# A two-layer vision block: the first mixer as straight code, with norms on ScalarE and the routing of one group inside the turn of the next

## The chip, the cores and the metric

The kernel runs on one core of a Trainium2 chip. The metric is the device time in microseconds of one execution. Five engines work at once: TensorE (PE; its weight loads are listed as PEld), VectorE (DVE), ScalarE (ACT), GpSimd (POOL) and SyncE (SP), which only issues DMAs. They meet through semaphores: one engine adds to a semaphore when an instruction is done, another waits until it has reached a number. Each engine works through its own list in order, so that whatever stands behind a waiting instruction waits too.

## The reference

The input is x, 16 images of 32 x 32 pixels with 96 channels. Two layers follow each other. Each has a token mixer and a feed-forward part with four experts, and both are added to their input.

```python
# layer 0, mixer (what this change is about)
xn = layernorm(x, eps 1e-6)
# along the rows of the image, and again along its columns:
y    = xn @ W1.T + b1                     # 96 -> 2 numbers per pixel
z    = grouped_mix(y, W2, b2, 8)          # 1024 logits for each column (row)
attn = softmax(z.reshape(..., 32, 32))    # a 32x32 matrix for each column (row)
h, w = attn @ v                           # v: values
x = x + projection of (pixel's own product + h + w)
# layer 0, feed-forward: 4 experts, the best 2 per pixel
g = softmax(layernorm(x, eps 1e-5) @ gate_w + gate_b);  keep 2, renormalise
x = x + sum over the two of  g_e * (gelu(xn @ w1[e] + b1[e]) @ w2[e] + b2[e])
# layer 1: a state-space mixer with a 3x3 convolution, then such a feed-forward
```

## The kernel before, in words

A *group* is four images. The 128 partitions hold 4 images x 32 image columns; the free dimension holds the 32 image rows, each with 96 channels and 8 more columns (the gate scores, the two gates, mean, reciprocal deviation, pixel number). All four groups stay in SBUF as `held_rows` (called `residual` in the profile); `xr` is its first 96 columns, `xsc` its first 100. Work on 4 image rows is a *quad*; a group has NQ = 8 quads.

**First mixer.** For each group VectorE computes 32 row sums (L408), GpSimd raises the variance to the power -1/2 (L424), VectorE normalises 32 rows (L376), TensorE transposes them (L981) and multiplies them by `rhs0`, 208 columns wide: 100 value columns, 100 columns of the pixel's own product, 4 columns for the logits and 4 scores (L996). ScalarE evacuates both (L782, L790). VectorE prepares the 2 + 2 mixing columns (L1605 to L1607), transposes the values in blocks of 32 (L1609) and adds the own product to the rows (L1612). TensorE makes the logits of the two directions, m = 0 and m = 1 (L1006). For each m VectorE takes the largest (L1616) and subtracts it (L1617), ScalarE takes the exponential (L795), VectorE sums, inverts, multiplies and transposes (L1619 to L1622). TensorE then applies the matrices with 32x32 products on quarters of its array, 8 quads for m = 0, whose results ScalarE evacuates, and 8 quads for m = 1, which VectorE adds to the rows (L1021, L1629). Last, VectorE transposes the column result (L1634) and adds it (L1635). On TensorE, ScalarE and VectorE the groups are a hardware loop (`Fori`). VectorE computes the row sums of group g+1 ahead of the adds of group g and normalises its rows between them. TensorE's transposes of group g+1 come after all mixing of group g. GpSimd splits the expert weights into two parts after each power (`expert_parts`), two of eight at a time, and SyncE writes them to memory.

**Routing.** When the mixer has ended, `stage_end` is raised. SyncE loads tables (L524, L525). For each group VectorE computes 32 row sums (L1668 to L1676), GpSimd the power (L627), VectorE the scores, the choice of two of four experts and the gates (`gated`, L1687 to L1728, with one exponential on ScalarE, L802), TensorE the ranks of the tokens (L1034, L1035), and VectorE the slots (`placed`, L1735 to L1743). Then GpSimd starts 32 scatters, one per image row (L632), that write the rows into the region of their expert pair in memory. The last row sums give the plan, by which SyncE writes fill rows (L532) and ScalarE loads the weights of the first tiles (L825). The order on VectorE is: row sums 0 and 1, then for each g gating, placing, row sums g+2. GpSimd's is: powers 0 and 1, then for each g the scatters, and the power of g+2 behind them.

**Expert tiles, second mixer, expert tiles.** SyncE waits for all scatters (L539) and loads the first tile of 512 tokens (L548). 74 tiles follow, then the second mixer, whose norms are on ScalarE already (L916) and which routes as it goes (scatters L738), then 74 tiles again.

Of the kernel before, what the change touches and what calls it, by code (L numbers as in the profile page):

```python
# [5 lines left out]
ALU = mybir.AluOpType  # L6
ACT = mybir.ActivationFunctionType
AX = mybir.AxisListType
# [5 lines left out]
P = 128  # L14
# [11 lines left out]
NV = 2 * DS + 2 * E0 + NEXP  # L26
# [46 lines left out]
CHAIN_MIX0 = 54  # L73


# [6 lines left out]
class Chain:  # L82
# [16 lines left out]

    def enter(self, i, per):  # L100
        self.start = self.base + self.n
        self.base, self.n = i * per + self.start, 0

    def leave(self, rounds, per):
        assert self.n == per, (self.n, per)
        self.base, self.n = self.start + rounds * per, 0


def metaformer(nc, inp, out):
    with ExitStack() as ctx:  # L110
# [44 lines left out]
        ids = xn_flat[:, 0:P].bitcast(I32)  # L155
        pad_rows = xn_flat[:, P:P + Q * ROW].rearrange("p (q n) -> p q n", q=Q)
# [28 lines left out]
        top[0] = 0  # L185
        wc = part(D + 1)
# [4 lines left out]
        xt0 = part(2 * BANK)  # L191
        vc = part(SIDE, NV)
        vh = part(SIDE, DS)
        oh = early[:, 2 * (WROW - 2):2 * (WROW - 2) + SIDE * DS].rearrange("p (a b) -> p a b", b=DS)
        gate_end = 2 * (WROW - 2) + SIDE * DS
        gwt0, gtmp0 = (early[:, gate_end + n * NEXP * D:gate_end + (n + 1) * NEXP * D].rearrange("p (e d) -> p e d", d=D) for n in range(2))
# [3 lines left out]
        row_max = part(SIDE)  # L200
# [7 lines left out]


        top[0] = 0  # L210
        plan = part(3, TILES).bitcast(I32)
        counts = part(NPAIR).bitcast(I32)
        plan_end = top[0]
# [16 lines left out]
        slot = part(G, SIDE).bitcast(U32)  # L230
# [8 lines left out]
        table_end = top[0]  # L239
# [7 lines left out]
        top[0] = max(top[0], table_end)  # L247
# [70 lines left out]
        m_ln, m_b01_pe, m_b01_ev = sem("m_ln"), sem("m_b01_pe"), sem("m_b01_ev")  # L318
        m_v_pe, m_v_ev, m_yb, m_yt_pe, m_yt_ev = (sem(n) for n in ("m_v_pe", "m_v_ev", "m_yb", "m_yt_pe", "m_yt_ev"))
        m_z_pe, m_sub, m_exp, m_at, m_w_pe, m_w_add = (sem(n) for n in ("m_z_pe", "m_sub", "m_exp", "m_at", "m_w_pe", "m_w_add"))  # L320

# [45 lines left out]
        def layer_norm(dve, ch, src, dst, n, width, which_eps, count, ready, part=None, own=None, rows=None):  # L367
            if part != 1:
                row_stats(dve, ch, src, n, width, which_eps, own or token_norm)
            if part == 0:  # L370
                return
            _, mom, _, has_rstd = own or token_norm
            dve.wait_ge(has_rstd, count)
            mo = mom[:, :, 0:n]
            for r in rows or range(n):
                i = dve.tensor_scalar(dst(r), src(r), mo[:, 0, r:r + 1], mo[:, 5, r:r + 1], ALU.subtract, ALU.mult)  # L376
                if ready is not None and (r + 1) % Q == 0:
                    i.then_inc(ready, 1)

# [24 lines left out]

        def row_stats(dve, ch, src, n, width, which_eps, own):
            sums, mom, has_var, _ = own
            for r in range(n):
                i = dve.bn_stats(sums[:, r, :], src(r))  # L408
                ch.done(i)
            ch.wait()  # L410
            sv = sums[:, 0:n, :]
            mo = mom[:, :, 0:n]
            ch.done(dve.tensor_tensor(mo[:, 0, :], sv[:, :, 1], sv[:, :, 4], ALU.add))
            ch.done(dve.tensor_tensor(mo[:, 1, :], sv[:, :, 1], sv[:, :, 4], ALU.subtract))
            ch.link(dve.tensor_tensor(mo[:, 2, :], sv[:, :, 2], sv[:, :, 5], ALU.add))
            ch.done(dve.tensor_scalar(mo[:, 0, :], mo[:, 0, :], 0.5, None, ALU.mult))
            ch.link(dve.tensor_tensor(mo[:, 1, :], mo[:, 1, :], mo[:, 1, :], ALU.mult))
            ch.link(dve.scalar_tensor_tensor(mo[:, 3, :], mo[:, 1, :], width / 4.0, mo[:, 2, :], ALU.mult, ALU.add))
            dve.tensor_scalar(mo[:, 4, :], mo[:, 3, :], 1.0 / width, which_eps, ALU.mult, ALU.add).then_inc(has_var, 1)

        def rstd(pool, n, count, own=None):
            _, mom, has_var, has_rstd = own or token_norm
            pool.wait_ge(has_var, count)
            pool.tensor_tensor(mom[:, 5, 0:n], mom[:, 4, 0:n], half_neg[:, 0:n], ALU.pow).then_inc(has_rstd, 1)  # L424

# [49 lines left out]
        def _(sp_):  # L475
            sp_.dma_start(consts[:, :], inp["consts"]).then_inc(const_in, 16)
            for g in range(G):
# [5 lines left out]
                if g == 0:  # L483
# [5 lines left out]
                    sp_.dma_start(rhs0[0:D + 1, 2 * DS:2 * DS + 2 * E0], inp["W1T"]).then_inc(mix_in, 16)  # L489
# [4 lines left out]
                    for m in range(2):  # L494
                        for c in range(SEG):
                            sp_.dma_start(w2z[8 * c:8 * c + 8, m, c * P:(c + 1) * P], inp["W2T"][m, c]).then_inc(mix_in, 16)
                        sp_.dma_start(w2z[64:65, m, :], inp["b2z"][m]).then_inc(mix_in, 16)
# [25 lines left out]
            def route_inputs():  # L523
                sp_.dma_start(route_consts, inp["route"]).then_inc(rc_in, 16)  # L524
                sp_.dma_start(ids, inp["ids"]).then_inc(rc_in, 16)  # L525

            def pads(l):
                sp_.wait_ge(rt["plan"], l + 1)
                sp_.wait_ge(pads_set, l + 1)
# [72 lines left out]
        def _(pool):  # L602
# [21 lines left out]
            def route():  # L624
# [16 lines left out]
                for g in range(G):  # L641
                    scatter(g)
                    if g + 2 < G:
                        powers(g + 2)
# [1226 lines left out]
```

## Time and profile before

| | us |
|---|---|
| median of three timed runs | 2229.65 (2222.31 to 2231.4) |
| the profiled execution | 2230.16, its span 2228.3, mean granted TensorE clock 0.882 |
| first mixer | 0 to 295 |
| routing | 295 to 496 |
| all the rest | 496 to 2228 |

| engine | busy us | share of the span |
|---|---|---|
| PE | 1744.2 | 78% |
| DVE | 1616.2 | 73% |
| ACT | 1108.5 | 50% |
| POOL | 1278.5 | 57% |

The shares are means over stages with different limits; the change touches the first two stages alone. A granted clock of 1 is 2.4 GHz, 0.50 is 1.2 GHz.

### The profile page before, as it was taken

The numbers are of one execution on the slowest core, as the hardware profiler recorded it, in microseconds if no ns is written. First come the engines' busy times: TensorE is split into PE (matmuls) and PEld (weight loads), VectorE is DVE, ScalarE is ACT, GpSimd is POOL, SyncE is SP. The second block draws the span as 40 slices with busy tenths as digits, with TensorE's granted clock in tenths as the row PEclk, the third lists the DMA queues.
The fourth block names the chain that finished last, engine by engine and source line by source line (L and its number), as shares of the span: only waits on it lengthen the run. The fifth ranks groups of instructions, "written<-read, shape, count | busy, mean of one in ns | idle before, by whom it ended". The sixth has DMA issues, their size and how long they took to land.

```text
span 2228.3 us, 65452 instructions
## 1 busy us (share of the span) xinstructions
PE 1744.2 (78%) x25602; PEld 1397.1 (63%) x25602; DVE 1616.2 (73%) x5205; ACT 1108.5 (50%) x2124; POOL 1278.5 (57%) x1346
## 2 busy tenths in 40 slices
PE   3566610009999994899999999999999936999997
PEld 2445510007777773788878777877788724777775
DVE  3877883206777776578898989898989864777775
ACT  2223300007777774565555555545554315777775
POOL 2210147764787776344546565656666664777776
PEclk9767765559999997899999999999999857999998
DMA  9200001315555554400000000000000014555553
GB/s 146 72 23 2 25 18 37 128 54 160 181 182 187 190 191 100 60 4 3 3 3 11 11 10 11 11 11 10 10 10 12 12 39 163 189 182 192 185 184 107
DMA packets 95635, 174.31 MB, mean 78 GB/s; under 512 B 53602, under 2 KB 66939, under 8 KB 95348
## 3 DMA queue, kind: packets, MB, share of 16 engines
q10 hardware_dynamic: 21312, 102.00, 13.8%
q1 hardware_dynamic: 56372, 42.14, 8.3%
q0 software_dynamic: 17664, 26.27, 3.5%
q8 instruction: 189, 3.10, 0.6%
q14 instruction: 98, 0.80, 0.1%
HBM read 134.99 MB, written 37.31 MB: 77 GB/s over the span
## 4 chain that ended last, share of the span: by engine, by line
PE 53%; DVE 22%; issue 11%; POOL 8%; ACT 4%; DMA 1%; SPq 1%; DVEq 0%; ACTq 0%; POOLq 0%
PE ps L1026 10%; PE ps L1027 9%; PE ps L1028 9%; PE ps L1118 6%; POOL rows L632 6%; PE ps L1153 3%; PE ps L1167 2%; PE ps L1076 2%; PE ps L996 2%; PE ps L1189 1%; PE ps L1048 1%; ACT rounded L870 1%; PE ps L1164 1%; PE ps L1172 1%; PE ps L1121 1%
## 5 line engine op out<-in xcount | busy, mean ns | idle before, releaser
L1026 PE MATMUL ps<-rounded 97*128 97x512 f32 (+2 forms) x952 | 394.0, 414 | 4.5 <-DVE rounded L1770 2.8
L1027 PE MATMUL ps<-rounded 97*128 97x512 f32 (+2 forms) x952 | 377.0, 396 | 0.0
L1028 PE MATMUL ps<-rounded 97*128 97x512 f32 (+2 forms) x952 | 376.4, 395 | 0.0
L1118 PE MATMUL ps<-rounded 128*128 128x224 f32 (+1 forms) x2256 | 353.6, 299 | 4.4 <-ACT rounded L870 4.4
L848 ACT ACTIVATE rounded<-ps 128x512 fp32r<-128x512 f32 x444 | 267.2, 602 | 162.2 <-PE ps L1028 154.7
L1118 PEld LDWEIGHTS ps<-rounded 128*128 128x128 f32 x2256 | 307.9, 200 | 38.7 <-issue 8.8
L1805 DVE TENSOR_TENSOR rounded<-arena,rounded 128x512 fp32r<-128x512 f32 x296 | 222.0, 750 | 136.2 <-ACT arena L849 136.0
L664 POOL TENSOR_TENSOR rounded<-arena,rounded 128x512 fp32r<-128x512 f32 x148 | 192.7, 1302 | 160.9 <-ACT arena L849 157.9
L849 ACT ACTIVATE arena<-ps 128x512 f32<-128x512 f32 x444 | 267.1, 602 | 0.0
L710 POOL TENSOR_TENSOR w<-arena,consts 128x384 f32<-128x384 f32 x128 | 107.7, 841 | 219.8 <-DVE arena L1327 219.8
L1026 PEld LDWEIGHTS ps<-rounded 97*128 97x128 f32 (+2 forms) x952 | 166.7, 175 | 57.8 <-issue 10.4
L1028 PEld LDWEIGHTS ps<-rounded 97*128 97x128 f32 (+2 forms) x952 | 166.6, 175 | 55.6 <-issue 0.2
L1027 PEld LDWEIGHTS ps<-rounded 97*128 97x128 f32 (+2 forms) x952 | 168.8, 177 | 43.3
L1784 DVE SCALAR_TENSOR_TENSOR arena<-ps,arena 128x96 f32<-128x96 f32 x592 | 146.4, 309 | 60.4 <-PE ps L1076 60.2
L655 POOL DMA_INDIRECT after_ffn<-arena x148 | 161.9, 1094 | 35.6 <-issue 30.4
L655 POOL DMA_INDIRECT out<-arena x148 | 156.2, 1055 | 35.6 <-issue 28.7
L870 ACT CAST rounded<-rounded 96x992 fp32r<-96x992 f32 (+2 forms) x192 | 155.5, 810 | 6.6 <-DVE rounded L1331 3.9
L632 POOL DMA_INDIRECT rows<-residual,arena x128 | 123.6, 966 | 42.8 <-issue 38.4
L738 POOL DMA_INDIRECT rows<-residual,w x128 | 128.7, 1005 | 32.2 <-issue 28.8
L1765 DVE TENSOR_SCALAR arena<-arena 128x96 f32<-128x96 f32 x296 | 79.2, 333 | 86.9 <-DMA arena<-rows 68.1
L1167 PEld LDWEIGHTS ps<-arena 32*32 32x32 f32 x12288 | 133.3, 105 | 12.4 <-issue 1.4
L1048 PE MATMUL ps<-consts,arena 128*96 128x128 f32 x296 | 45.7, 278 | 113.9 <-DVE arena L1765 81.3
(309 smaller groups left out, 3816.0 us busy)
## 6 DMA issues: line engine op xcount, KB each, us to landing
rounded<-weights_by_expert ACTq DMA_DIRECT2D x148, 673.0 KB, 4.6
arena<-rows SPq DMA_DIRECT2D x74, 208.0 KB, 2.7
residual<-in_x SPq DMA_DIRECT2D x16, 384.0 KB, 7.1
weights_by_expert<-rounded SPq DMA_DIRECT2D x8, 672.0 KB, 3.2
residual<-after_ffn SPq DMA_DIRECT2D x12, 384.0 KB, 6.8
rows<-xn SPq DMA_DIRECT2D x17, 208.0 KB, 8.3
after_ffn<-arena POOLq DMA_INDIRECT x148
out<-arena POOLq DMA_INDIRECT x148
```

What stands on the lines that cost most here:

```text
L632: pool.indirect_dma_start(rows, bass.IndirectOffsetOnAxis(ap=slot[:, g, h:h + 1], axis=0), held_rows[:, g, h, :], None).then_inc(r_out[g % ...
L655: pool.indirect_dma_start(to, bass.IndirectOffsetOnAxis(ap=mine[:, COL_ID:COL_ID + 1].bitcast(U32), axis=0), mine[:, 0:D], None, bounds_ch ...
L664: pool.tensor_tensor(hidr[:, 1, c, :], hid[:, step % HIDS, :], hidr[:, 0, c, :].bitcast(F32), ALU.subtract).then_inc(f["low_pool"], 1)
L848: act.activation(hidr[:, 0, c, :], bank(UPS[step % len(UPS)]), ACT.Gelu)
L849: act.activation(hid[:, step % HIDS, :], bank(UPS[step % len(UPS)]), ACT.Gelu).then_inc(f["gelu"], 1)
L870: return act.copy(dst[:, :, :, to], src[:, :, :, frm].bitcast(F32))
L1026: pe.matmul(dst, left[0], right[0], start=start, stop=False)
L1027: pe.matmul(dst, left[1], right[0], start=False, stop=False)
L1028: return pe.matmul(dst, left[0], right[1], start=False, stop=stop)
L1118: pe.matmul(dst[:, 0:w], x3[:, x_part, n, slot, tokens], wtap[:, w_part, n, y + 1, 0:w], start=(y == 0 and n == x_part == w_part == 0), st ...
L1167: ins = pe.matmul(bank(5)[pb, n * HD:(n + 1) * HD], mm[pb, i % 2, n, :], xdt[pb, c % 2, j, n, :], start=True, stop=True)
L1805: dve.tensor_tensor(hidr[:, 1, c, :], hid[:, step % HIDS, :], hidr[:, 0, c, :].bitcast(F32), ALU.subtract).then_inc(f["low"], 1)
```

## The change

The first mixer and the routing become one piece of straight code.

- **Norms.** VectorE computes signed sums (the mean times -1); GpSimd makes the power and one product; ScalarE normalises all 32 rows of a group with a scale and a bias per row. `xt0` now holds a whole group.
- **Products.** The value product is 108 columns wide (`VC`: values, 4 logit columns, 4 scores). The other 100 columns are multiplied in the row mixing: each row of a quad is one product of full height and then four quarter products into the same PSUM columns. VectorE's separate addition (L1612) is gone. 
- **Order.** TensorE: for each group column mixing, row mixing, then columns, values and logits of the next group. ScalarE takes one exponential, evacuates two quads, takes the other, evacuates the rest, then norms, columns and values of the next group. Row sums are one group further ahead.
- **Routing of g-1 in the turn of g.** Row sums between the two softmax halves, gating before the row adds, placing after the first two; the ranks on TensorE after the second quad. GpSimd's scatters have the other powers put between them at fixed places. Its first norms and the weight splitting are reordered. The tables are loaded at the start.
- Waits at the start are split: the first products wait for 8 small loads and not for all 26.

```diff
@@ ScalarE
+            def normalise(g):
+                act.wait_ge(rstd_ready, g + 1)
+                need(act, m_t_pe, g * NQ)
+                for h in range(SIDE):
+                    ins = act.activation(xn[:, h, :], xr[:, g, h, :], ACT.Identity, bias=moments[:, 1, h:h + 1], scale=moments[:, 5, h:h + 1])
...
+            for g in range(G):
+                softmax_exp(g, 0)
+                mixed_columns(g, 0)
+                mixed_columns(g, 1)
+                softmax_exp(g, 1)
+                for q in range(2, NQ):
+                    mixed_columns(g, q)
+                if g:
+                    gate_exp(g - 1)
+                if g + 1 < G:
+                    normalise(g + 1)
+                    columns_and_values(g + 1)
+                    mixing_columns(g + 1)
+            gate_exp(G - 1)
@@ TensorE
+            def mix_rows(g, q):
+                k = g * NQ + q
+                if q == 0:
+                    pe.wait_ge(m_at, 2 * g + 2)
+                    pe.wait_ge(m_v_ev, k + NQ)
+                elif q >= 2:
+                    pe.wait_ge(m_w_add, k - 1)
+                apart()
+                for i in range(Q):
+                    h, dst = Q * q + i, bank(2 + q % 2)[:, i * DS:(i + 1) * DS]
+                    pe.matmul(dst, xt0[0:D + 1, h * P:(h + 1) * P], rhs0[0:D + 1, VC:NV], start=True, stop=False)
+                    for pb in quarter:
+                        ins = pe.matmul(dst[pb, :], at[pb, 1, :, h], vc[pb, h, 0:DS], start=False, stop=True)
+                ins.then_inc(m_w_pe, 1)
...
+            for g in range(G):
+                for q in range(NQ):
+                    mix_columns(g, q)
+                for q in range(NQ):
+                    mix_rows(g, q)
+                    if q == 1 and g:
+                        ranks_of(g - 1)
+                if g + 1 < G:
+                    columns_and_values(g + 1)
+                    mixing_weights(g + 1)
+            ranks_of(G - 1)
@@ GpSimd
+            norm_of(0)
...
+            norm_of(1)
+            parts_of(0, 1, 2, 3)
+            norm_of(2)
+            parts_of(4, 5)
+            powers(0)
+            parts_of(6, 7)
             for g in range(G):
-                rstd(pool, SIDE, g + 1)
-                for k in (2 * g, 2 * g + 1):
-                    expert_parts(k // NEXP, k % NEXP)
-            route()
+                cuts = (22, 26) if g == 0 else (26, 26) if g == 1 else (16, 16)
+                scatter_group(g, range(0, cuts[0]))
+                if g == 0:
+                    norm_of(3)
+                scatter_group(g, range(*cuts))
+                if g + 1 < G:
+                    powers(g + 1)
+                scatter_group(g, range(cuts[1], SIDE))
@@ VectorE
+            def values(g):
+                dve.wait_ge(m_v_ev, (g + 1) * NQ)
...
+            for g in range(G):
+                peaks(g, 0)
+                below_peaks(g, 0)
+                peaks(g, 1)
+                shares(g, 0)
+                below_peaks(g, 1)
+                if g:
+                    row_sums(g - 1)
+                shares(g, 1)
+                if g:
+                    gated(g - 1)
+                add_rows(g, range(2))
+                if g:
+                    placed(g - 1)
+                add_rows(g, range(2, NQ))
+                add_columns(g)
+                if g + 1 < G:
+                    values(g + 1)
+                if g + 2 < G:
+                    next_sums(g + 2)
+            dve.sem_inc(stage_end, 1)
+            row_sums(G - 1)
+            gated(G - 1)
+            placed(G - 1)
+            planned(carry, rc0)
```

`row_sums`, `gated` and `placed` have the same instructions as before. `peaks` is L1616, `below_peaks` L1617, `shares` L1619 to L1622 for one m, `add_rows` L1629, `add_columns` L1634 and L1635, `values` L1605 to L1611 without L1612, `next_sums` the 32 row sums of a later group.

## Rows read from the trace of the kernel before

**Rows 1.** Stretches of all engines: busy us (instructions) of each, clock, DMA share, GB/s.

```profile
0.00:295.00 295.00, 159.08 (x2474) 132.10 (x2474) 214.34 (x414) 79.57 (x144) 49.29 (x47) 0.79 0.24 51
295.00:496.00 201.00, 6.56 (x16) 4.56 (x16) 68.15 (x349) 1.25 (x4) 146.19 (x135) 0.50 0.18 62
```

**Rows 2.** Timeline of the scatters: start, us, engine, line, operation, idle before it.

```profile
320.84 1.19 POOL L632 DMA_INDIRECT rows<-residual,arena  x1 [4.39 <-DVEq L1744]
...
361.31 5.50 POOL L627 TENSOR_TENSOR residual<-arena,half_neg 128x32 f32<-128x32 f32 x1
...
492.98 0.95 POOL L632 DMA_INDIRECT rows<-residual,arena  x1 [0.30 <-issue]
...
496.01 42.89 SPq L548 DMA_DIRECT2D arena<-rows  x7
```

**Rows 3.** Timeline of VectorE in the routing.

```profile
310.73 0.40 DVE L1687 TENSOR_TENSOR arena<-residual 128x128 f32<-128x128 f32 x1
...
317.74 0.55 DVE L1735 TENSOR_TENSOR_SCAN arena<-xn,ps 128x192 f32<-128x192 f32 x1
...
320.63 5.21 DVE L1668 BATCH_NORM_STATS2 arena<-residual 128x6 f32<-128x96 f32 x32
...
327.05 0.40 DVE L1687 TENSOR_TENSOR arena<-residual 128x128 f32<-128x128 f32 x1
```

**Rows 4.** A stretch of all engines in the first loads (columns as Rows 1).

```profile
12.00:15.00 3.00, 0.00 (x0) 0.00 (x0) 0.00 (x0) 0.00 (x0) 0.00 (x0) 1.00 0.31 72
```

**Rows 5.** Timeline of VectorE in the first group.

```profile
19.48 0.21 DVE L1586 COPY arena<-arena 96x96 f32<-96x96 f32 x1 [17.44 <-DMA arena<-in_b2z]
...
25.11 5.21 DVE L408 BATCH_NORM_STATS2 stats<-residual 128x6 f32<-128x96 f32 x32 [0.24 <-DVE arena L365]
...
56.92 0.22 DVE L1605 COPY arena<-arena 128x64 f32<-128x64 f32 x1 [11.94 <-ACT arena L790]
```

**Rows 6.** Timeline of ScalarE in the second mixer, four norms (one alone: 450 ns).

```profile
1326.18 1.54 ACT L916 ACTIVATE xn<-residual,moments 128x96 f32<-128x96 f32 x4
```

**Rows 7.** Timeline of VectorE in a softmax of group 3.

```profile
261.36 1.22 DVE L1616 TENSOR_REDUCE arena<-ps 128x32 f32<-128x1024 f32 x1
...
269.04 1.19 DVE L1616 TENSOR_REDUCE arena<-ps 128x32 f32<-128x1024 f32 x1
```

**Rows 8.** Groups by line, 0 to 540 us: count, busy us, mean ns, idle before.

```profile
L376 DVE TENSOR_SCALAR xn<-residual,moments 128x96 f32 (+1 forms) x128 | 38.7, 368 | 19.3 <-POOL moments L424 19.3
...
L1634 DVE STREAM_TRANSPOSE arena<-early 128x3200 f32<-128x3200 f32 x4 | 23.9, 5968 | 0.0
...
L1629 DVE TENSOR_TENSOR residual<-residual,ps 128x400 f32 (+1 forms) x32 | 17.7, 562 | 3.8 <-PE ps L1021 3.4
...
L1635 DVE TENSOR_TENSOR residual<-residual,arena 128x3200 f32 (+1 forms) x4 | 14.0, 3492 | 0.1
```

**Rows 9.** Timeline of TensorE in the second mixer.

```profile
1300.29 0.64 PE L1099 MATMUL ps<-consts,xn 128*96 128x128 f32 x4
1300.87 0.26 PE L1150 MATMUL ps<-arena 16*32 16x32 f32 x8
1301.06 0.91 PE L1153 MATMUL ps<-w,consts 128*128 128x384 f32 x2
...
1305.07 2.03 PE L1189 MATMUL ps<-arena 96*128 96x100 f32 x16
1307.03 0.26 PE L1150 MATMUL ps<-arena 16*32 16x32 f32 x8
```

**Rows 10.** Timeline of TensorE in the last row mixing.

```profile
279.49 4.98 PE L1021 MATMUL ps<-arena 32*32 32x100 f32 x192 [0.16 <-DVE residual L1629]
```

**Rows 11.** A stretch of L1021 alone: PE busy, PEld busy, clock, DMA share, GB/s.

```profile
204.00:208.00 4.00, 2.59 (x64) 2.56 (x64) 0.50 0.00 0
```

**Rows 12.** The page's costliest groups: the scatters of both mixers.

```profile
L632 POOL DMA_INDIRECT rows<-residual,arena x128 | 123.6, 966 | 42.8 <-issue 38.4
L738 POOL DMA_INDIRECT rows<-residual,w x128 | 128.7, 1005 | 32.2 <-issue 28.8
```

More of the change, by code:

```diff
@@ L185, in metaformer @@
         top[0] = 0
+        plan = part(3, TILES).bitcast(I32)
+        counts = part(NPAIR).bitcast(I32)
+        plan_end = top[0]
+        slot = part(G, SIDE).bitcast(U32)
         wc = part(D + 1)
@@ new lines, in to_columns, with values @@
+            def to_columns(g, q):
+                k = g * NQ + q
+                pe.wait_ge(m_ln, k + 1)
+                if g and q == 0:
+                    pe.wait_ge(m_h_ev, k)
+                need(pe, m_t_ev, k - 1)
+                for i in range(Q):
+                    ins = pe.transpose(bank(q % 2)[0:D, i * P:(i + 1) * P], xn[:, Q * q + i, :], ident)
+                ins.then_inc(m_t_pe, 1)
+            def values(g, q):
+                k = g * NQ + q
+                pe.wait_ge(m_t_ev, k + 1)
+                need(pe, m_v_ev, k - 1)
+                if q == 0:
+                    need(pe, m_w_add, k)
+                for i in range(Q):
+                    h = Q * q + i
+                    ins = pe.matmul(bank(2 + q % 2)[:, i * VC:(i + 1) * VC], xt0[0:D + 1, h * P:(h + 1) * P], rhs0[0:D + 1, 0:VC], start=True, stop=True)
+                ins.then_inc(m_v_pe, 1)
@@ L998, in _, with columns_and_values, mixing_weights @@
+            def columns_and_values(g):
+                for q in range(NQ + 1):
+                    if q < NQ:
+                        to_columns(g, q)
+                    if q:
+                        values(g, q - 1)
+            def mixing_weights(g):
                 pe.wait_ge(m_yb, g + 1)
@@ L1594, in _ @@
+            ch.link(dve.tensor_tensor(rhs0[D:D + 1, VC:VC + D], bank(5)[D:D + 1, 0:D], bo[D:D + 1, :], ALU.add))
+            times_gates(dve, ch, rhs0[0:D + 1, VC + D:NV], rhs0[0:D + 1, VC:VC + D], gwt0, gtmp0)
             dve.sem_inc(prep_done, 1)
-            dve.sem_inc(m_w_add, NQ)
-            def normalise(g, part=None, rows=None):
-                if part != 1:
-                    dve.wait_ge(x_in, g * 64 + 64)
-                layer_norm(dve, ch, lambda r: xr[:, g, r, :], lambda r: xn[:, r, :], SIDE, D, 1e-6, g + 1, m_ln, part, rows=rows)
@@ new lines, in logits, with peaks, below_peaks @@
+            def logits(m):
+                return bank(6 - 2 * m, 2).rearrange("p (i j) -> p i j", j=SIDE)
+            def peaks(g, m):
+                dve.wait_ge(m_z_pe, g * 2 + m + 1)
+                ch.done(dve.tensor_reduce(row_max[:, m, :], logits(m), AX.X, ALU.max))
+            def below_peaks(g, m):
+                ch.wait()
+                need(dve, m_at, g * 2 + m)
+                dve.tensor_tensor(sc[:, :, :], logits(m), row_max[:, m, :].unsqueeze(2).to_broadcast([P, SIDE, SIDE]), ALU.subtract).then_inc(m_sub, 1)
@@ new lines, in shares, with add_rows @@
+            def shares(g, m):
+                dve.wait_ge(m_exp, g * 2 + m + 1)
+                ch.link(dve.tensor_reduce(row_sum, at[:, m, :, :], AX.X, ALU.add))
+                ch.link(dve.reciprocal(row_inv, row_sum))
+                ch.link(dve.tensor_tensor(sc[:, :, :], at[:, m, :, :], row_inv.unsqueeze(2).to_broadcast([P, SIDE, SIDE]), ALU.mult))
+                dve.transpose(at[:, m, :, :], sc[:, :, :]).then_inc(m_at, 1)
+            def add_rows(g, some):
+                ch.wait()
+                for q in some:
+                    dve.wait_ge(m_w_pe, g * NQ + q + 1)
```

505 lines of the change are left out of this document (214 added, 291 removed).

## The prediction

> **What bounds the kernel now.** I first cut the span into stages [rows 1]. To 295 us the first mixer runs; VectorE is busy for 214 of these 295 us, TensorE for 159 at a mean granted clock of 0.79. From 295 to 496 us the routing runs, and there only GpSimd works (146 of 201 us); TensorE does 6.6 us. Both stages are whole in the chain of waits, and the expert tiles begin only when the second has ended. I then read GpSimd's timeline in the second stage [rows 2]: the first of 128 scatters starts at 320.84, 32 of them take 40.5 us (1.265 each), a power of 5.5 us stands between two groups, and the last starts at 492.98. SyncE's load of the first tile follows at 496.01. So 320.8 to 493.9 is one engine's queue, which needs nothing but slots. VectorE has the slots of a group after 32 row sums, gating and placing: 6.4, 7.0 and 2.9 us [rows 3].
>
> **The change, part by part.** The sum is made on the profiled execution (2230.16 us; the median of the three timed runs, 2229.65, is 0.5 less). The stage after the scatters is not touched and is moved as a block; the price is therefore where the last scatter ends, against 493.9.
>
> *Start.* The waits for the mixing weights no longer stand ahead of the first row sums. DMA's share falls to 0.31 in 12 to 15 us, so the first group's rows are there at about 12.9 [rows 4]. Sums 6.4 [rows 3], power 5.5 [rows 2] and GpSimd's short product some 0.3: 25.1. The weights' preparation (5.6 us on VectorE, 19.48 to 25.11 [rows 5]) lies under the power. The longer memset of the ones (four times as many elements, some 3.6 us) ends before 12.9.
>
> *Norms on ScalarE.* Four in 1.54 us with 0.45 for one alone is 0.363 from start to start [rows 6]; 32 make 11.6 us, where VectorE takes 0.37 for one at most, in all 38.7 for 128 [rows 8]. ScalarE is slower or equal, but in groups 1 to 3 its norms lie beside TensorE's row mixing. In group 0 nothing covers them: 36.7. ScalarE evacuates nothing until all 32 are done.
>
> *Columns and values.* Four transposes take 0.58 at most [rows 9]. A value product has two instructions now for 108 columns; I take the 0.1225 of the output projection, 16 in 1.96 us (nearest shape: 96x128 weights, 100 columns; 1305.07 to 1307.03 in [rows 9]), so 0.98 for a quad. 8 x 1.56 = 12.5 us, after which ScalarE's last evacuation needs 0.5: 50. Before, the same stretch ends at 56.92 [rows 5]. Then copies and scores 1.5 and the transpose of values 5.9 (same size as L1634 in [rows 8]): the first logits are read at 58 (call it P0; before, it is 67.6). TensorE's logits lie under that transpose.
>
> *A turn without routing (group 0).* Reading, subtracting and the first shares take 7.7 [rows 7], and 7.9 with the second peaks taken inside ScalarE's exponential. Column mixing runs from there to P+17, because ScalarE puts two evacuations ahead of the second exponential. Row mixing: a quad of the present one is 32 instructions at 0.0259 (192 in 4.98), 0.83 to 0.85 us [rows 10]. To it come eight instructions of full height, 0.98, the product moved here from the value stage; the 3.5 us addition on VectorE (same size as L1635 in [rows 8]) that brought it in is gone. The array changes between full and quarter height twice per row: between 1300.29 and 1300.87 stand four transposes and one such change, so 0.09 is left for it if a transpose takes 0.1225; the eight quarter products after it take 0.19 with the change back [rows 9]. No row shows the change alone; between 0 and 0.36 a row for both, I take 0.15. A quad is 0.85 + 0.98 + 0.6 = 2.43 at full clock. The present mixing runs at low clock at its start (two quads in 2.59 us at 0.50 [rows 11]), so I take 2.7. Eight quads: the turn's mixing ends at T0 = 58 + 17 + 21.6 = 96.6.
> The Trainium skill says that changing the tiling mode "drains the TensorE" (TensorEngine Tiling (Array Packing), Key Properties) and gives no price; it speaks against putting full products between the quarter ones. At my upper bound it costs 26 quads x 0.84 = 22 us more than the 0.15 taken, at the lower 16 us less.
>
> *From T to the next P.* Last add 0.6, column transpose 5.97 and addition 3.49 [rows 8]: T+10.1. Meanwhile TensorE makes columns and values of the next group (12.5) and ScalarE evacuates: T+13. The order on VectorE decides it, since its values follow the column addition: VectorE idles 3 us. Then 1.5 + 5.9, and sums of the group after next 6.4 [rows 3]: P' = T+27, and T+20.6 where no sums are left (group 2's turn). P1 = 123.6.
>
> *A turn with routing.* Two peaks, two subtractions and the first shares end at P+9.1 [rows 7]; row sums P+15.5; second shares P+19.6, and TensorE starts row mixing. Gating waits for GpSimd's power (5.5 after P+15.5), so it runs P+21.1 to P+28.1. VectorE only then adds quads 0 and 1 (0.57 each [rows 8]), and TensorE's third quad waits for the first of these adds: it stands from about P+26.5 to P+28.8. This is the new wait, 2 us; behind it stand the six remaining quads and everything of the next group. Placing (2.9) lies under quads 2 and 3, the ranks (1.5 us) before the stall. T = P + 28.8 + 6 x 2.7 = P+45. So T1 168.6, P2 195.6, T2 240.6, P3 261.2, T3 306.2. The mixer ends at T3 + 10.1 = 316, later than before (295), with three groups routed.
>
> *GpSimd's queue.* Slots of group 0 at P1+32.2 = 156. The sum of the third norm waits for P2 behind 22 scatters (done 184): idle 12, harmless. The power of group 1 is reached at 206.5, due 211. The power of group 2 stands behind 26 scatters of group 1, from 228 to 261, due 276.7: 16 us of slack. Half of group 2 is scattered from 293.4 to 313.6. None of the cuts holds VectorE up.
>
> *Tail.* Row sums 316.3 + 6.4 = 322.7, power 328.2. Then scatters run without a gap: 16 + 32 at 1.265 and 0.4 for the first ones [rows 2]; the last slots (328.2 + 9.9 = 338) are there before 348.6. End 389.3. The plan (some 7 us) and the fill rows by SyncE lie under it. Saved: 493.9 - 389.3 = 104.6 us. **2230.2 - 104.6 = 2125.6.**
>
> **Rivals.**
> *A, half clock.* TensorE waits for VectorE three times a turn, and its granted clock stays at 0.50. A quad costs 1.3 [rows 11] + 1.96 + 0.6 = 3.9: 26 quads x 1.2 = 31 more, 2157; with the upper price of changes 2179. For it: the clock is 0.50 at the start of a mixing [rows 11]. Against: the mixer's mean is 0.79 [rows 1], and TensorE gets more to do in one piece.
> *B, full clock and free changes.* A quad is 1.83: 26 x 0.87 = 23 less, 2103.
> *C, slower than before.* The scatters now run beside VectorE's largest operations. If GpSimd cannot write the descriptors of a scatter while VectorE holds what both need, their pitch p grows. GpSimd's work from 156 is 128 p + 22 (four powers and products), and it ends after 493.9 once p is over 2.47 us; at 2.7 the kernel takes 2260. Against it: the pitch is the same 1.265 while VectorE works without a gap (320 to 343) as after it [rows 2], and in the second mixer one takes 1.005 in place of 0.966 [rows 12]. The 48 scatters of the tail have an idle VectorE.
> The Trainium skill describes just this stall, of descriptors written by GpSimd while VectorE is in a two-port mode (SBUF — State Buffer, "two separate sides"). By that rule C would happen here; the two rows above do not show it for these operations.
> *D, nothing in the right place.* If the row sums, gating and placing of g-1 found no idle VectorE, they would be added to each turn; that is already counted (16.3 us a turn), which is why the mixer does not get shorter.
>
> **How the numbers follow.** Forecast case (a quad of 2.2 to 3.3, 2113 to 2141): 0.68; A 0.14; B 0.14; C 0.04. Predicted 2125. Range: B's end and a few us for the start to A without the dearest changes, 2097 to 2160. Under 0.5% (11 us) a measurement of this kernel tells no change. Only C gives no gain: faster 0.95, same 0.01, slower 0.04.
>
> **What would show it.** In the changed profile: scatters of group 0 start at 150 to 165, the last ends at 375 to 405; between, GpSimd's powers wait for VectorE and not the reverse. Row mixing takes 2.2 to 3.3 us a quad, with a stall of TensorE on an add after the second quad. VectorE is busy over 80% from 58 to 316. The stage from the first tile to the end is as long as now (1732 us). Wrong would be: scatters at over 1.4 us pitch, a turn of over 80 or under 60 us, or a later stage that changes by more than 10 us.

## The result, and the profile after

The changed kernel takes 2195.01 us (median of 4 runs, 2187.78 to 2195.9) against 2226.49 (median of 4, 2222.31 to 2231.4): a ratio of 0.985, 95% interval 0.9825 to 0.9875. It is faster by 31 us (1.5%) and not by 105, and lies outside the range of 2097 to 2160. The profiled execution took 2195.41 us (span 2193.4, mean clock 0.869).

The first thing to look at are stretches of all engines (columns as [rows 1]): the row mixing of group 0, the last six quads of group 1's, group 2's, and the tail. The fourth group's is like the second's.

```profile
80.00:118.00 38.00, 38.00 (x334) 22.89 (x324) 4.08 (x8) 11.96 (x33) 0.00 (x0) 0.50 0.01 1
178.00:206.00 28.00, 28.00 (x242) 16.87 (x243) 5.53 (x15) 3.21 (x9) 19.08 (x20) 0.50 0.12 37
258.00:296.00 38.00, 38.00 (x318) 23.61 (x318) 13.82 (x52) 11.78 (x33) 25.33 (x27) 0.50 0.11 36
384.00:457.00 73.00, 1.62 (x4) 1.14 (x4) 22.09 (x103) 0.31 (x1) 51.67 (x49) 0.50 0.32 109
```

TensorE is busy for all of the first three stretches, and the granted clock is 0.50 (1.2 GHz). VectorE, which the old mixer was bound by (214 of 295 us, [rows 1]), is busy for 4 of 38 us in group 0's row mixing, and for 14 of 38 with the routing in group 2's. The bound has changed hands. TensorE's timeline shows one row after another (start, us, engine, line, operation):

```profile
94.45 0.75 PE L1031 MATMUL ps<-arena,early 97*128 97x100 f32 x2
95.13 0.56 PE L1033 MATMUL ps<-arena 32*32 32x100 f32 x8
95.61 0.75 PE L1031 MATMUL ps<-arena,early 97*128 97x100 f32 x2
```

A row is the full-height product L1031 (0.68 from its start to the next line's) and the quarter products L1033 (0.48): 1.16 to 1.17 us, so 4.67 a quad where 2.7 was forecast. Only the first rows of two mixings were faster: in group 1 the clock was 1.00 until 166.5 and in group 3 until 337.2, 1.4 and 1.0 us after the first row product, and then 0.50. Where six quads stand in a row (the last six of a routing turn) nothing else lies between them.

The start, the wait of TensorE on the first add, and the tail, from the timelines of ScalarE, VectorE, TensorE, GpSimd and SyncE:

```profile
25.06 11.56 ACT L745 ACTIVATE xn<-residual,moments 128x96 f32<-128x96 f32 x32 [23.04 <-POOL moments L381]
...
59.99 1.22 DVE L1652 TENSOR_REDUCE arena<-ps 128x32 f32<-128x1024 f32 x1
...
79.14 1.38 PE L1018 MATMUL ps<-arena 32*32 32x100 f32 x25 [3.62 <-issue]
...
177.78 0.72 PE L1031 MATMUL ps<-arena,early 97*128 97x100 f32 x2 [2.43 <-DVE residual L1671]
...
181.14 1.22 POOL L585 DMA_INDIRECT rows<-residual,arena  x1 [8.85 <-DVEq L1778]
...
374.15 0.57 DVE L1671 TENSOR_TENSOR residual<-residual,ps 128x400 f32<-128x400 f32 x1 [4.09 <-PE ps L1033]
...
456.25 0.96 POOL L585 DMA_INDIRECT rows<-residual,arena  x1 [0.30 <-issue]
...
459.30 42.36 SPq L502 DMA_DIRECT2D arena<-rows  x7
```

The first tile is loaded at 459.30, against 496.01 [rows 2]: 36.7 us earlier, of which the whole execution shows 34.8.

### The profile page after: what moved, and what is told of

The parts are those of the page before. It is cut to its first block, busy times and chain, and to the rows that moved or that the text cites. A ratio compares the mean times of both kernels' runs of the same rounds, so it can differ in the third digit from the quotient of the medians.

```text
span 2193.4 us, 65534 instructions
## 1 busy us (share of the span) xinstructions
PE 1866.8 (85%) x25858; PEld 1458.6 (66%) x25858; DVE 1575.9 (72%) x5073; ACT 1133.2 (52%) x2217; POOL 1284.8 (59%) x1350
## 4 chain that ended last, share of the span: by engine, by line
PE 58%; DVE 24%; issue 7%; POOL 4%; ACT 4%; DMA 1%; DVEq 0%; SPq 0%; ACTq 0%; POOLq 0%
PE ps L1062 10%; PE ps L1063 9%; PE ps L1064 9%; PE ps L1143 6%; PE ps L1031 4%; PE ps L1178 3%; PE ps L1033 3%; PE ps L1192 2%; PE ps L1102 2%; POOL rows L585 2%; PE ps L981 2%; PE ps L1074 2%; ACT rounded L859 1%; PE ps L1214 1%; PE ps L1189 1%
## 5 line engine op out<-in xcount | busy, mean ns | idle before, releaser
L378 POOL TENSOR_TENSOR moments<-moments,half_neg 128x4 f32<-128x4 f32 (+1 forms) x36 | 54.7, 1520 | 155.2 <-DVE moments L373 135.3
L1192 PE MATMUL ps<-arena 32*32 32x16 f32 x12288 | 132.8, 181 | 1.4 <-issue 0.9
```

Of the source, the lines that this page charges most:

```text
L1192: ins = pe.matmul(bank(5)[pb, n * HD:(n + 1) * HD], mm[pb, i % 2, n, :], xdt[pb, c % 2, j, n, :], start=True, stop=True)
```

## The experiments

All but the third and the fifth compute the full result. A change of height is a step from full-height products (97 rows of the array) to quarter-height ones (32) or back. M and R are the two theories on record for the clock: M says that the alternation of full and quarter height keeps it at 0.50, R that TensorE's earlier waiting does and alternation costs its own time only. Ratios are against runs of the kernel before on the same chip.

**1 and 2: fewer changes of height.** Four (two) full products in a row, then their 16 (8) quarter products; the bank is started by its first product alone.

```diff
-                for i in range(Q):
-                    ... full product of row i
-                    ... 4 quarter products of row i
+                for first in range(0, Q, 4):          # experiment 2: 2
+                    for i in range(first, first + 4):
+                        ... full product of row i, start=(i == 0)
+                    for i in range(first, first + 4):
+                        ... 4 quarter products of row i
```

> Row mixing with the four full-height products of a quad first and its 16 quarter products after them: two changes between full and quarter height a quad in place of eight. Same products, same sums. Theory M (the changes empty the array, and that keeps the granted clock at 0.50): the clock in the row mixing rises over 0.8, a quad falls from 4.67 us to 2.0 to 2.5, some 26 quads count, so about 60 us less: 2130 to 2145. Theory R (the clock is at 0.50 because TensorE waited before; the changes only cost their own time): the clock stays at 0.50, a quad costs 4 x 0.50 + 4 x 0.325 + 0.34 = 3.6 us, 27 us less: about 2168.

> The same with groups of two rows: four changes a quad. M: between the kernel after the change and e1, the clock partly up, a quad 2.5 to 3.7, 2140 to 2170. R: clock at 0.50, a quad 4.0 us, 2178.

Measured: 2152.87 us, ratio 0.9627 (0.9588 to 0.9666), and 2159.86 us, 0.9677 (0.9619 to 0.9734). TensorE in the first, then in the second:

```profile
97.86 2.03 PE L1032 MATMUL ps<-arena,early 97*128 97x100 f32 x8
99.81 1.56 PE L1036 MATMUL ps<-arena 32*32 32x100 f32 x32
101.30 2.03 PE L1032 MATMUL ps<-arena,early 97*128 97x100 f32 x8
```

```profile
95.75 1.18 PE L1032 MATMUL ps<-arena,early 97*128 97x100 f32 x4
96.86 0.89 PE L1036 MATMUL ps<-arena 32*32 32x100 f32 x16
97.68 1.17 PE L1032 MATMUL ps<-arena,early 97*128 97x100 f32 x4
```

The same products take 3.44 us a quad with 2 changes of height, 3.86 with 4 (twice 1.93), 4.67 with 8. That is a straight line: 3.03 + 0.205 for each change. Two stretches of the first, in the row mixings of groups 0 and 3:

```profile
81.00:108.00 27.00, 27.00 (x320) 23.44 (x319) 4.00 (x7) 11.68 (x33) 0.00 (x0) 0.50 0.01 1
314.00:334.00 20.00, 19.32 (x240) 16.57 (x240) 6.25 (x15) 0.00 (x0) 12.59 (x14) 0.55 0.12 36
```

The clock is 0.50 in the gapless part of all eight row mixings of the two kernels, but for the first 1.5 to 1.8 us of two of them. That is R's clock. The times are not R's: the first lies between what M and R gave, the second in M's range. The first tile of experiment 1 is loaded at 418.51, 40.8 us earlier. Of this 33 lie in the turns up to the last row add, where 26 quads x 1.23 gives 32. Six more lie behind it, where the values of the next group run at a higher mean clock (0.81 in each group against 0.63 to 0.72): R left this out.

**3: own products left out** (the full product of each row, so the rows lack it and the routing works on other numbers).

> Row mixing without the full-height products (the pixel's own product and its share of the gate scores are left out): quarter products alone, no change of height. A quad is 0.85 us at full and 1.3 at half clock, VectorE's add 0.57. Both theories: some 26 x 3.4 = 88 us less, 2100 to 2115. They differ in the clock: M over 0.8 in the row mixing, R 0.50.

Measured: 2106.28 us, 0.9434 (0.9409 to 0.9459), in the range on record. Its first tile, and the clock in the row mixing of group 0 and in the last six quads of group 1's:

```profile
366.44 41.97 SPq L502 DMA_DIRECT2D arena<-rows  x7
```

```profile
79.00:88.00 9.00, 8.23 (x272) 7.70 (x265) 3.99 (x7) 8.55 (x24) 0.00 (x0) 0.81 0.02 4
150.00:159.00 9.00, 7.43 (x193) 7.01 (x193) 6.09 (x15) 3.99 (x12) 4.09 (x4) 0.57 0.06 20
```

The clock is M's in group 0 and close to R's in the others. The first tile is loaded 92.9 us earlier (459.30 - 366.44); the rest takes 1739 us against 1734. So the product that was put into the row mixing costs 93 us there. In its old place it cost 14 us of additions on VectorE (L1612, four of 3.49 us) and TensorE's part of the value stage, which no run separates.

**4: own products among the values**, eight banks of them a group, added to the rows by VectorE quad by quad ahead of the mixing; the row mixing has quarter products alone.

```diff
+            def own_products(g, q): ...      # called behind values(g, q), banks 5 to 7
+            def own_adds(g, some): ...       # VectorE, 8 additions of 128x400
-                    ... full product of row i in mix_rows
```

> The own products are moved out of the row mixing to the values of the same rows, four full-height products a quad into other banks, and VectorE adds them from there (8 adds of 0.57 us a group). Nothing is left out. M: the stretch of columns and values grows from 12.5 to about 20 us at full clock, the row mixing falls to VectorE's adds and 0.85 us a quad: turn 69 us in place of 91, 2110 to 2130. R: the longer stretch is at half clock too and takes some 32 us: 2150 or more.

Measured: 2154.67 us, 0.9652 (0.962 to 0.9683), R's side. But its clock fits neither theory. Three stretches of its trace: group 0's mixing, then columns, values and own products of group 1, then the same of group 2:

```profile
86.00:103.00 17.00, 15.79 (x515) 14.30 (x507) 9.33 (x14) 13.37 (x34) 0.00 (x0) 1.00 0.02 4
106.00:138.00 32.00, 31.59 (x152) 31.41 (x152) 10.23 (x9) 7.88 (x16) 0.00 (x0) 0.52 0.00 1
194.00:212.00 18.00, 17.53 (x157) 17.11 (x155) 13.49 (x11) 8.01 (x16) 14.19 (x13) 1.00 0.12 37
```

Full-height work without a gap ran at 0.52 in one group (106 to 138) and at 1.00 in the next (194 to 212), so the same work gets either level with no alternation in it. The four own products of a quad cost 1.69 us at 0.50 (107.65 to 109.34) and 0.88 at 1.00 (197.92 to 198.80) in their new place, where the next values wait behind them.

**5: quarter products left out** of the row mixing.

> The quarter-height products of the row mixing are left out (so the mixed rows lack their own row's part, and the routing works on other numbers); the full-height own products stay, so the row mixing has no change of height. Question: is the granted clock 0.50 in the row mixing because the array changes height there, or because TensorE stood waiting before it? Theory M (changes keep it low): within a few us of the start of row mixing the clock is 1.00 and a quad takes about 0.98 us, as the values do. Theory R (earlier waits keep it low): the clock stays at 0.50 through the eight quads and one takes about 1.7 (1.69 for four own products in the fourth experiment at 0.50). On time: some 2100 by M, 2105 to 2115 by R, so the clock rows decide, not the time.

Measured: 2109.59 us (one run), in R's range. The row mixing of group 0:

```profile
78.38 13.16 PE L1031 MATMUL ps<-arena,early 97*128 97x100 f32 x64
```

```profile
79.00:91.00 12.00, 12.00 (x60) 12.00 (x60) 3.99 (x7) 11.44 (x32) 0.00 (x0) 0.51 0.01 1
```

A quad takes 1.71 at 0.50 with nothing alternating, and the clock stays at 0.50 to the end of all four row mixings. M as the only cause has fallen.

**6: alternation at a high clock.** Experiment 4, whose clock is 1.00 at its first mixing, with a full-height product before each row's quarter products again, into a bank that nobody reads.

```diff
+                    pe.matmul(bank(4)[:, 0:DS], xt0[...], rhs0[0:D + 1, VC:NV], start=True, stop=True)
                     for pb in quarter: ...
```

> The fourth experiment (own products ahead, among the values; its granted clock was 1.00 from 60 to 104 us, through the first group's column and row mixing) with the alternation put back: before every row's four quarter products one full-height product into a bank that nobody reads, 8 changes a quad. The clock is thus at 1.00 when alternation begins. Theory M: alternation pulls the clock down within a few us of the start of the first group's row mixing, and a quad then takes 4.67 as in the changed kernel. Theory R: the clock stays at 1.00 through most of that row mixing, and a quad takes 0.98 + 1.06 + 8 changes; that shows the price of a change at full clock, 0.1 each (quad 2.85) if it goes with the clock, 0.2 (3.65) if it doesn't. Time 2225 by M, about 2215 by R.

Measured: 2237.77 us (one run). Two row mixings of this one kernel, of group 0 and of group 1:

```profile
97.00:116.00 19.00, 19.00 (x267) 13.17 (x262) 4.00 (x7) 8.60 (x25) 0.00 (x0) 1.00 0.01 2
178.00:210.00 32.00, 29.49 (x248) 18.02 (x244) 9.61 (x33) 7.71 (x22) 18.58 (x20) 0.50 0.14 48
```

```profile
97.75 0.47 PE L1043 MATMUL ps<-arena,early 97*128 97x100 f32 x2
...
98.48 0.47 PE L1043 MATMUL ps<-arena,early 97*128 97x100 f32 x2
```

```profile
182.93 0.56 PE L1045 MATMUL ps<-arena 32*32 32x100 f32 x8
183.42 0.75 PE L1043 MATMUL ps<-arena,early 97*128 97x100 f32 x2
```

In group 0 the clock stays at 1.00 under full alternation until its end: a row is 0.725 and a quad 2.90. In the others it falls to 0.50 within 2 us of the first row, and a quad takes 4.67. So alternation need not pull the clock down. The time is above both forecasts (2225 and 2215). The clock of 1.00 from 60 us on that the expectation starts from is wrong for its first part: the own products before 70 us take 1.7 us a quad (60.24 to 61.94), as at 0.50. It is the row mixing, from 94 us, that ran at full clock.

**7: routing after the mixer again**, with the changed mixer as it is.

```diff
-                if g:
-                    row_sums(g - 1)
                 shares(g, 1)
-                if g:
-                    gated(g - 1)
...
+            row_sums(0); row_sums(1)
+            for g in range(G):
+                gated(g); placed(g); row_sums(g + 2)   # and the scatters behind
```

> The changed kernel with its mixer as it is, but row sums, gating, placing and scatters of all groups after the mixer, as in the kernel before. It splits the 31 us gained into what the overlap gave and what the new mixer took. Theory: a turn with routing loses row sums (6.4), gating (7 to 10.6) and the wait of TensorE for VectorE's adds, some 18 us a turn for three turns, so the mixer ends some 50 us earlier than 384, at 330 to 340, against 295 before: the new mixer alone is 35 to 45 us slower. After it the routing needs the 201 us that it took before (first sums 6.4, power 5.5, gating and placing 10, then 128 scatters at 1.265, with no norm between): last scatter at 525 to 540, kernel 2260 to 2280, slower than before. Rival: the new mixer costs nothing by itself (ends at 295 or before) and the loss lies in the overlap: then 2225 to 2235.

Measured: 2264.73 us, 1.0144 (1.0111 to 1.0176). The end of its mixer and its first tile:

```profile
333.56 3.49 DVE L1672 TENSOR_TENSOR residual<-residual,arena 128x3200 f32<-128x3200 f32 x1
...
535.00 4.78 SPq L502 DMA_DIRECT2D arena<-rows  x5
```

The new mixer alone ends at 337 instead of 295, 42 us later, and the first tile comes 39 later than before (535.0 - 496.0). Overlapping the routing gives 535.0 - 459.3 = 75.7 us. The rival on record, that the new mixer costs nothing by itself, has fallen. Stretches of its row mixings, group by group:

```profile
86.00:118.00 32.00, 32.00 (x276) 19.32 (x279) 3.87 (x7) 7.06 (x20) 0.00 (x0) 0.50 0.00 1
168.00:183.00 15.00, 15.00 (x211) 10.30 (x210) 2.85 (x5) 6.15 (x18) 0.00 (x0) 1.00 0.00 1
234.00:266.00 32.00, 32.00 (x276) 19.31 (x280) 3.94 (x7) 8.32 (x24) 0.00 (x0) 0.50 0.00 1
307.00:327.00 20.00, 20.00 (x279) 13.77 (x278) 3.85 (x7) 0.00 (x0) 0.00 (x0) 1.00 0.01 2
```

Groups 0 and 2 ran at 0.50 (4.67 a quad), groups 1 and 3 at 1.00 (2.90), from the same instructions. So 16 quads x 1.77 = 28 us of the comparison is clock. With them at 0.50, as in the changed kernel, the new mixer would be some 70 us slower than the old (an estimate), and the overlap would be worth some 75.7 + 28 = 104. That holds if the overlap is not itself what brings 0.50. It may be: the row sums that it puts between the softmax halves make TensorE wait ahead of the row mixing. The first row product of group 1, in the changed kernel and in this one:

```profile
165.08 0.44 PE L1031 MATMUL ps<-arena,early 97*128 97x100 f32 x2 [3.59 <-DVE arena L1664]
```

```profile
162.69 0.44 PE L1027 MATMUL ps<-arena,early 97*128 97x100 f32 x2 [0.56 <-DVE arena L1659]
```

Both start at 1.00; the first mixing is at 0.50 after 1.4 us, the second stays at 1.00. My 18 us a turn on record was wrong: 384.1 - 337 - 28 = 19 for all three turns, some 6 each; the ends came out as expected by luck, since the clock made up for it.

**8: eight rows apart, splitting early.** Eight full products, then 32 quarter products, over two banks of four (one change a quad); and GpSimd's `parts_of(4 to 7)` ahead of `norm_of(2)`.

```diff
-            parts_of(0, 1, 2, 3)
+            parts_of(0, 1, 2, 3, 4, 5, 6, 7)
             norm_of(2)
-            parts_of(4, 5)
             powers(0)
-            parts_of(6, 7)
```

> The full result, with eight own products in a row and then 32 quarter products over two banks (one change a quad), and the splitting of expert weights 4 to 7 on GpSimd put ahead of the third norm, so that it no longer lies beside the first gating. At 0.50 a quad took 3.03 + 0.205 for each change (4.67 with 8, 3.86 with 4, 3.44 with 2), so 3.24 here: 26 quads x 1.43 = 37 less than the changed kernel, 5 less than the first experiment's 42. The first gating takes 7.0 in place of 10.6: 3.6 less. By Theory R: 2140 to 2148 (clock 0.50 in row mixing). By Theory M with the clock held by the changes alone: with one change a quad the clock rises within the row mixing, a quad takes about 1.9, and 2110 to 2125.

Measured: 2101.6 us (5 runs, 2096.14 to 2109.06), 0.943 (0.9406 to 0.9454). This is the best version, 127 us below the kernel before. TensorE in group 0:

```profile
79.23 3.74 PE L1032 MATMUL ps<-arena,early 97*128 97x100 f32 x16
...
85.72 3.73 PE L1032 MATMUL ps<-arena,early 97*128 97x100 f32 x16
...
98.21 2.03 PE L1032 MATMUL ps<-arena,early 97*128 97x100 f32 x16
...
100.17 1.61 PE L1037 MATMUL ps<-arena 32*32 32x100 f32 x64
```

A quad takes 3.245 at 0.50 (6.49 for two), as expected from the line, and 1.75 at 1.00 (98.21 to 101.71, where the next transposes begin). Here the clock rose within the row mixing in all four groups, in groups 1 to 3 after 3 to 7 us at 0.50. A stretch of group 1:

```profile
149.00:164.00 15.00, 14.15 (x299) 13.01 (x302) 11.93 (x50) 11.78 (x33) 3.19 (x4) 0.89 0.03 9
```

The time is below both theories' ranges, since the clock came back in the mixing. M called for that, but what brought it back isn't shown: with no change at all (experiment 5) it stayed at 0.50. The first tile is loaded at 371.27, 88 us earlier than in the changed kernel. The experiment has two edits, and no run tells the shares apart.

**9 and 10: spare products in TensorE's waits**, into banks that nobody reads: 28 ahead of the column mixing, 8 ahead of the row mixing, 12 and 6 around the ranks, in the changed kernel (9); 28, 8 and 6 in that of experiment 8 (10).

```diff
+            def spare(b, n):
+                for i in range(n):
+                    pe.matmul(bank(b)[:, 0:DS], xt0[...i...], rhs0[0:D + 1, VC:NV], start=True, stop=True)
```

> The changed kernel with only spare work added: where TensorE waits for VectorE in a turn it first computes full-height products into banks that nobody reads: 28 ahead of the column mixing, 8 ahead of the row mixing, 12 and 6 around the ranks (the last three only in turns with routing). The row mixing itself keeps its 8 changes a quad. Theory H (the level that the clock has when a row mixing begins decides: it stays at 1.00 while TensorE is kept at work, and at 0.50 under alternation): most row mixings now run at 1.00, a quad takes 2.90 as in the sixth experiment, 26 quads x 1.77 = 46 less, some of it given back by spare products that end late (up to 3 us a turn): 2150 to 2165. With the clock left low (the spare products change nothing): 2200 to 2215, slower than the changed kernel. My recorded forecast of 2125 had the quad at 2.7.

> The eighth experiment (eight rows apart, early splitting) with spare products in TensorE's waits (28, 8 and 6). Theory H: its row mixings were at 0.50 for about half of their time (3.24 a quad against 1.75 at 1.00, and VectorE's adds behind); the gain left is about 12 quads x 1.5 = 18 at most, less what the spare products delay: 2085 to 2100. If the spare products only delay: 2105 to 2115.

Measured: 2185.65 us, 0.9775 (0.9744 to 0.9807), and 2109.07 us, 0.9438 (0.9406 to 0.9471). The gapless part of the four row mixings of experiment 9:

```profile
84.00:104.00 20.00, 20.00 (x279) 13.87 (x280) 4.00 (x7) 9.13 (x26) 0.00 (x0) 1.00 0.01 2
172.00:195.00 23.00, 23.00 (x201) 13.87 (x201) 2.60 (x6) 0.00 (x0) 17.51 (x19) 0.50 0.13 44
264.00:287.00 23.00, 23.00 (x201) 13.74 (x201) 2.60 (x5) 0.00 (x0) 17.51 (x19) 0.50 0.13 43
343.00:358.00 15.00, 14.97 (x210) 10.24 (x208) 2.85 (x5) 0.00 (x0) 11.34 (x13) 1.00 0.14 43
```

Two mixings are now at 1.00 with 2.90 a quad, two still at 0.50 with 4.67. The first tile comes at 443.12, 16 us earlier. From the first reading of the logits to the last row add, groups 0 and 3 take 12.1 and 6.5 us less than in the changed kernel, groups 1 and 2, where the clock fell, take 4.1 and 7.6 more (64.6 and 66.0 against 60.5 and 58.4). The time lies in neither range on record. The ratio is below that of the change (0.985), but theory H is not borne out: the clock fell in groups 1 and 2 although TensorE was kept at work, and experiment 7 had two mixings at 1.00 with no spare product at all. In experiment 10 nothing is won in the whole (0.9438 against 0.943): the first tile is loaded at 365.82, 5.4 us earlier than in experiment 8, and what follows takes 10 us more.

## Why the prediction was wrong, step by step

Measured with the prediction's own marks: P is where VectorE first reads a group's logits, T where its last row add begins.

| step | forecast | measured | late by |
|---|---|---|---|
| P0 | 58 | 60.0 | 2.0 |
| P0 to T0 | 38.6 | 57.9 | 19.3 |
| T0 to P1 | 27 | 27.5 | 0.5 |
| P1 to T1 | 45 | 60.5 | 15.5 |
| T1 to P2 | 27 | 31.0 | 4.0 |
| P2 to T2 | 45 | 58.4 | 13.4 |
| T2 to P3 | 20.6 | 21.2 | 0.6 |
| P3 to T3 | 45 | 57.6 | 12.6 |
| T3 to the last scatter's end | 83.1 | 83.1 | 0.0 |

The sum is 67.9, and the last scatter ends at 457.2 instead of 389.3. With the 1.9 that the later stages took more that is the 69.8 between 2125.6 and 2195.4.

- **The failed step is the quad of the row mixing.** "A quad is 0.85 + 0.98 + 0.6 = 2.43 at full clock ... I take 2.7." It took 4.67: 26 quads on the path x 1.97 = 51 of the 68 us (the few first rows at 1.00 left aside). Two terms in it were wrong. *The change of height*: I took 0.15 a row for both changes, from a bound of 0.36. It is 0.41 a row at 0.50 (experiments 1 and 2), and at 1.00 (2.90 - 1.75) / 7 = 0.164 a change, 0.33 a row (experiments 6 and 8). The price at 1.00 comes from two points alone. With it a quad at full clock takes 2.90, not 2.43: without any change it would be 1.59, where the sum had 1.83. The row that I weighed, one change beside four transposes [rows 9], left 0.09 for a change and was not measured in a run of them. *The clock*: the allowance of 0.27 stood for a start at 0.50 [rows 11]; but for 1.4 and 1.0 us the whole of each row mixing ran at it, 1.77 a quad more than at 1.00. So 1.77 of the 1.97 is clock: at full clock the 2.7 would have been only 0.20 short, since the 0.27 and the 0.24 too much for the products made up for most of the changes.
- **Rival A was the true case**, with the upper price of the changes (4.7 a quad, 2179 us), to which I gave 0.14; the measured time is 16 us above even that. "Against: the mixer's mean is 0.79 [rows 1]" was the wrong argument: a mean over the stage before said nothing of a stretch that did not exist in it. A's reason, that TensorE waits for VectorE, fits most row mixings (next but one point) and isn't shown as the cause.
- The Trainium skill's "drains the TensorE" (TensorEngine Tiling (Array Packing), Key Properties) spoke against this edit, and the runs agree with it: 0.16 to 0.21 us for each change.
- **What sets the clock stays open.** Shown: five row mixings ran at 1.00 to their end with eight changes a quad (6, 7, 9), so alternation alone does not bring 0.50; it is not needed for it either (4, 5); and spare work in the waits does not prevent it (9). Once at 0.50 in a row mixing with eight changes a quad, the clock stayed there to the end, also over 38 us without a gap; so it did with four (2) and with none (5). With two (1) it did so but for 3.4 us in group 3, around a wait; with one (8) it rose within the mixing, four times in four. What goes with the level best is the longest wait of TensorE from the start of its column mixing to its first row product. There are 16 row mixings with eight changes a quad (changed kernel, 6, 7, 9). In nine that wait was 1.57 to 3.62 us, and the clock fell, at the latest 2 us after that product. In the five that stayed at 1.00 it was 1.48 us at most. The other two, groups 1 and 2 of experiment 9, fell with 0.97 and 1.16 us. No rule that fits all of these is offered, and no run changes this wait alone.
- **Group 0.** The quad apart, 3.4 us: the last column products waited 3.62 us (79.14) for nothing that the trace names. The DMA engines moved 98 GB/s meanwhile. The queue named "instruction" has one packet of 16 KB from 76.6 to 77.7 us; whether TensorE waited for it isn't shown.
- **Gating of group 0** took 10.6 us, not 7.0, because GpSimd's splitting of weights fell beside it. One operation of GpSimd, two of VectorE's beside it in group 0's gating, and the same two in group 1's:

```profile
166.91 1.04 POOL L428 TENSOR_TENSOR rounded<-w,rounded 97x384 fp32r<-97x384 f32 x1
...
167.13 0.98 DVE L1722 TENSOR_TENSOR arena<-arena,gate_b 128x128 f32<-128x128 f32 x1
...
169.44 1.65 DVE L1728 TENSOR_TENSOR arena<-arena 128x96 f32<-128x96 f32 x3
...
258.43 0.29 DVE L1722 TENSOR_TENSOR arena<-arena,gate_b 128x128 f32<-128x128 f32 x1
...
259.49 0.49 DVE L1728 TENSOR_TENSOR arena<-arena 128x96 f32<-128x96 f32 x3
```

  I had put GpSimd's queue beside VectorE and looked only at who waits for whom, not at operands. With the splitting moved away (experiment 8) the gating takes 7.1 us (148.65 to 155.79). The Trainium skill has VectorE and GpSimd share a port pair that one instruction holds whole, also when VectorE reads two inputs from SBUF and GpSimd reads SBUF too (SBUF — State Buffer, "two separate sides"); the 0.98 for 0.29 agrees.
- **T1 to P2**: values of the next group ran at a mean clock of 0.67 (206 to 224 us), and were ready at T+17.6, not T+13.
- **Right:** the norms on ScalarE (11.56 for 11.6), the stall on the first add (2.43 us for 2.3), the tail to 0.1 us, an unchanged later stage, and rival C's end: the scatters' pitch is 1.265 beside a busy VectorE (295.93 to 300.99, under the column transpose) as beside an idle one. "By that rule C would happen here" took a rule on two-port modes for one on all large operations of VectorE.
- **D** names 16.3 us a turn for the routing; the forecast's own sum has 6.4 (45 - 38.6), and some 6 were measured (7).
- **The signs** were clear: group 0's scatters start at 181 and not by 165, VectorE is busy for 58% of 58 to 316 us and not over 80%, and two of three turns take over 80 us (85.4, 91.5, 79.6).

So the change is two: an overlap worth 76 us and a mixer that takes 39 of them back, 36.7 net at the first tile, as measured with experiment 7. If the low clock is put down to the mixer alone, it is some 104 and 67 (an estimate), and 104 would be the size forecast for the whole change. The forecast had the new mixer no slower than the old. The own product in the row mixing was the loss in it (93 us, experiment 3, a part of them clock), and of that the eight changes of height a quad are the part that another loop order removes.

## What to carry to other kernels

When an edit puts work of another tile height between small products, price the change of height itself (here 0.16 to 0.21 us each, as dear as a quarter-height row at full clock), group by height, and count it 8 or 1 times. When a stage is cut off VectorE onto TensorE, price it at both granted clocks as cases of equal standing; the clock of a stage before is no evidence for a stretch of another make. Split a large change by moving one half back: experiment 7 showed at once that one half gave and the other took.

## What the runs showed of the hardware

- The cost of a change between full and quarter height goes down by a fifth where the clock doubles: 0.205 us at 0.50 (four kernels on a line) and 0.164 at 1.00 (two points), where a full-height product goes from 0.42 to 0.22 (experiment 4).
- The same gapless instructions got the clock 0.50 in some groups and 1.00 in others of one execution (experiment 7), which makes 4.67 or 2.90 of a quad. From the start of the column mixing to its first row product, TensorE's longest wait was 3.07 and 1.57 us in the groups at 0.50, and 0.56 us and none in those at 1.00.
- Quarter-height products after a full-height one in the same bank need no start of their own; a bank started once by its first product accumulates all four rows (the full results of experiments 1, 2 and 8).
- VectorE's 128x128 operations take up to 3.4 times as long beside GpSimd's operations on whole tiles (0.98 for 0.29), and no longer beside its scatters (0.29 at 258.43, between scatters at 258.11 and 259.61).
